# A two-layer transformer kernel on one core: smaller loads, a new instruction order, and query stacks transposed by DMA in the second layer

## The chip, the cores and the metric

The kernel runs on one core of one Trainium2 chip. The metric is the device time of one execution in microseconds. A core has TensorE (PE, matrix products and transposes into PSUM), VectorE (DVE), ScalarE (ACT), GpSimd (POOL) and SyncE (SP), which here only issues DMA transfers; each works through its own queue of instructions in order, and they wait for one another through semaphores.

## The reference

The input x is 8 blocks of 128 tokens by 128 features, the context is of the same shape. Two layers follow one another:

```
x = x + cross_attention_0(layernorm(x), ctx, mask[b])       # 16 heads of 8, mask of each block
x = x + bit_linear_ffn(layernorm(x))                         # 128 -> 512 (gate, up) -> 128, quantised
x = x + cross_attention_1(layernorm(x), ctx, mask shared)    # per-head weights, output bias
x = x + mixture_of_8_experts(layernorm(x))                   # all 8 computed, top 2 weighted
```

An attention computes q, k, v from the normalised x and from the context, the scores q k^T, sets masked ones to a very low value, and takes the softmax over keys and the product with v, then the output projection.

## The kernel before

A *unit* is one attention with the feed-forward part behind it, of one layer l and one block b: (l, b). There are 16, run in the order of UNIT_ORDER (line 71); n is a unit's place in it. Each unit is a list of steps such as `pe.max` or `dve.rk` (the engine, then the step), ATTENTION (line 75) and what STEPS adds for the layer. The function plan() (line 266) simulates the five queues with the costs in TIME (pitch and latency of each step), the buffer rings in SLOTS, the arrival times of loads in ARRIVES, and the ranks START and BIAS, and so fixes the order of each engine's instructions before the kernel is built. All engines then follow these orders, every step with waits for the steps it needs.

The scores need products of more precision than bf16 holds, so q and k are split into bf16 parts which lie side by side as a *stack*. For a unit these steps matter here:

- Keys: `pe.kv`, `act.kh`, `act.v`, `dve.rk`, `pool.km`, `pool.kl` fill kst (128 x 2048 bf16). `sp.ks` (line 566) turns it by a DMA transpose into kblk.
- Queries: layernorm (`dve.st`, `dve.ag`, `pool.pw`, `dve.nm`), `pe.xT`, `act.xT`, `pe.q`, `act.qh`, `dve.rq`, `pool.qm`, `pool.ql` fill qst (128 x 1024 bf16). `pe.qs` turns it in 8 TensorE transposes (line 708) into PSUM, and `act.qs` (line 850) copies it to qT.
- `pe.max` (lines 675, 677): the mask and the scores, 4 parts; `dve.max` (line 1063) takes their maximum over the keys. `dve.m1` to `dve.m3` write the maxima, split in three, into qst. `pe.qb` (again 8 transposes, line 708) and `act.qb` (line 850) make qmT, the shifted stack.
- `pe.exp` (lines 690, 692): shifted scores, with keys on the partitions; `act.exp` their exponential; `pe.pv`, `act.pv`, `pe.oT`, `dve.rd`, `dve.at`, `pe.aT`, `act.aT`, `pe.wo`, `dve.wo`: the output; `dve.fs` to `dve.fn`: the second layernorm.
- In layer 0, the quantised feed-forward; in layer 1 the experts: `pe.z` (line 826), `act.z`, `pe.y` (line 839), `dve.y` (line 1228), `pool.sum`, and `sp.out` (line 575), the store.
- `dve.mk` (lines 1043, 1044) casts the masks m0_i and m0T_i of one block.

Before the first unit, SyncE's queue holds the loads of x block 0, constants, x blocks 1 to 7, and the masks of blocks 0 and 1; ScalarE's queue holds the first layer's weights and the context. The rest of the loads stand behind the first four key transposes on SyncE (later_loads, line 535). SyncE issues everything in order, so a wait in its queue holds what stands behind it.

## Time and profile before

| | us |
|---|---|
| median of 3 runs (214.77 to 215.25) | 214.84 |
| profiled execution | 216.64 |
| its span, first to last instruction | 214.8 |
| TensorE busy | 196.6 |
| VectorE busy | 162.4 |
| ScalarE busy | 135.3 |
| GpSimd busy | 82.7 |

The span is what the trace covers; the 1.84 us by which the profiled execution is longer lie around it. Busy time of TensorE is from matmuls whose ends are modelled, so it shows whether the engine was supplied, not whether it ran at its peak.

### The profile page before, as it was taken

The numbers are of one execution on the slowest core, as the hardware profiler recorded it, in microseconds if no ns is written. First come the engines' busy times: TensorE is split into PE (matmuls) and PEld (weight loads), VectorE is DVE, ScalarE is ACT, GpSimd is POOL, SyncE is SP. The second block draws the span as 40 slices with busy tenths as digits, with TensorE's granted clock in tenths as the row PEclk, the third lists the DMA queues.
The fourth block names the chain that finished last, engine by engine and source line by source line (L and its number), as shares of the span: only waits on it lengthen the run. The fifth ranks groups of instructions, "written<-read, shape, count | busy, mean of one in ns | idle before, by whom it ended". The sixth has DMA issues, their size and how long they took to land.

```text
span 214.8 us, 6119 instructions
## 1 busy us (share of the span) xinstructions
PE 196.6 (92%) x2114; PEld 160.8 (75%) x2114; DVE 162.4 (76%) x608; ACT 135.3 (63%) x378; POOL 82.7 (38%) x197
## 2 busy tenths in 40 slices
PE   2487697999999999999999999999999999999992
PEld 0255474757766777777888988898979889999992
DVE  6458989999999999999987859966576736265225
ACT  3343466468868677766968579547955576566430
POOL 4494320432337544143520425438210604232532
PEclk9999889999999999999999999999999999999998
DMA  5849678504440724430080000400220000000000
GB/s 156 243 111 303 164 98 349 145 9 101 108 92 0 160 50 92 98 87 17 2 92 9 5 0 17 98 3 12 54 47 6 0 15 0 17 0 15 2 10 24
DMA packets 39747, 15.09 MB, mean 70 GB/s; under 512 B 34211, under 2 KB 38819, under 8 KB 39462
## 3 DMA queue, kind: packets, MB, share of 16 engines
q1 hardware_dynamic: 39142, 14.00, 27.7%
q10 hardware_dynamic: 576, 0.72, 1.0%
q8 instruction: 17, 0.28, 0.6%
q14 instruction: 12, 0.10, 0.1%
HBM read 5.80 MB, written 0.52 MB: 29 GB/s over the span
## 4 chain that ended last, share of the span: by engine, by line
PE 81%; DVE 7%; DMA 5%; issue 2%; SPq 2%; POOL 1%; ACT 1%; DVEq 0%; ACTq 0%
PE ps_B L826 14%; PE ps_A L839 12%; PE ps_O L756 7%; PE ps_B L690 7%; PE ps_A L675 6%; PE ps_B L692 6%; PE ps_Q L708 6%; PE ps_A L677 6%; DMA m0T_i<-in_mask0T 5%; PE ps_O L764 3%; PE ps_X L722 2%; PE ps_A L791 2%; PE ps_O L774 2%; PE ps_A L835 2%; PE ps_P L736 2%
## 5 line engine op out<-in xcount | busy, mean ns | idle before, releaser
L907 ACT ACTIVATE probs<-ps_B 128x512 f32<-128x512 f32 x64 | 36.5, 598 | 15.6 <-PE ps_B L692 14.8
L956 ACT ACTIVATE hid<-ps_B,b_sb 128x128 f32<-128x128 f32 x128 | 35.6, 378 | 15.3 <-PE ps_B L826 15.2
L1063 DVE TENSOR_REDUCE mx<-ps_A 128x4 f32<-128x512 f32 x64 | 42.0, 677 | 3.7 <-PE ps_A L677 3.7
L826 PE MATMUL ps_B<-mxT,w_sb 128*128 128x128 f32 x256 | 33.3, 278 | 0.0
L839 PEld LDWEIGHTS ps_A<-w_sb,hid 128*128 128x128 f32 x256 | 31.1, 192 | 0.6
L839 PE MATMUL ps_A<-w_sb,hid 128*128 128x128 f32 x256 | 31.2, 275 | 0.0
L826 PEld LDWEIGHTS ps_B<-mxT,w_sb 128*128 128x128 f32 x256 | 30.6, 192 | 0.5 <-issue 0.4
L654 POOL TENSOR_TENSOR yc<-yc 128x512 f32<-128x512 f32 (+2 forms) x21 | 17.3, 823 | 34.1 <-DVE yc L1228 33.0
L675 PE MATMUL ps_A<-m_b,id_b 128*128 128x512 bf16 x64 | 24.7, 385 | 2.4 <-DVE mx L1063 1.2
L692 PEld LDWEIGHTS ps_B<-qmT,kblk 118*128 118x128 bf16 x256 | 20.4, 100 | 8.6 <-issue 0.8
L692 PE MATMUL ps_B<-qmT,kblk 118*128 118x128 bf16 x256 | 25.5, 223 | 0.0
L677 PE MATMUL ps_A<-kblk,qT 112*128 112x256 bf16 x128 | 24.6, 273 | 0.0
L1228 DVE TENSOR_TENSOR yc<-ps_A,comb 128x512 f32<-128x512 f32 x16 | 11.0, 689 | 15.4 <-PE ps_A L839 15.3
L624 POOL CAST kst<-kr 128x128 bf16<-128x128 f32 x32 | 9.6, 328 | 30.1 <-DVE kr L1050 30.0
L708 PE MATMUL ps_Q<-id_b,qst 128*112 128x128 bf16 (+1 forms) x256 | 20.6, 225 | 0.3 <-ACT qT L850 0.2
L708 PEld LDWEIGHTS ps_Q<-id_b,qst 128*112 128x112 bf16 (+1 forms) x256 | 18.5, 136 | 2.4 <-issue 1.1
L590 POOL TENSOR_TENSOR ry<-hv,half 128x1 f32<-128x1 f32 x32 | 18.8, 586 | 2.7
L587 POOL TENSOR_SCALAR hv<-mv 128x1 f32<-128x1 f32 x32 | 7.1, 223 | 31.0 <-DVE mv L1111 27.0
L677 PEld LDWEIGHTS ps_A<-kblk,qT 112*128 112x128 bf16 x128 | 12.7, 99 | 8.4 <-issue 0.3
L722 PE MATMUL ps_X<-wkv_sb,ctx_sb 128*128 128x256 f32 x32 | 11.7, 450 | 6.8 <-DMA ctx_sb<-in_ctxT 4.0
L756 PE MATMUL ps_O<-probs,v_sb 128*9 128x128 f32 x512 | 17.0, 273 | 0.7 <-issue 0.7
L756 PEld LDWEIGHTS ps_O<-probs,v_sb 128*9 128x9 f32 x512 | 12.4, 90 | 3.1 <-issue 2.1
(135 smaller groups left out, 391.5 us busy)
## 6 DMA issues: line engine op xcount, KB each, us to landing
w_sb<-in_m1T SPq DMA_DIRECT2D x1, 1024.0 KB, 6.2
w_sb<-in_m2T SPq DMA_DIRECT2D x1, 1024.0 KB, 8.1
out_y<-out_sb SPq DMA_DIRECT2D x8, 64.0 KB, 1.5
x_sb<-in_x SPq DMA_DIRECT2D x1, 448.0 KB, 6.7
ctx_sb<-in_ctxT ACTq DMA_DIRECT2D x1, 448.0 KB, 5.5
m_i<-in_mask SPq DMA_DIRECT2D x1, 384.0 KB, 4.2
m0T_i<-in_mask0T SPq DMA_DIRECT2D x1, 384.0 KB, 5.0
kblk<-kst SPq DMA_TRANSPOSE x16, 3.7
```

The lines of the kernel that those rows point to most:

```text
L590: ends(pool.tensor_tensor(ry[:, k, b, :], hv[:, k, b, 0:1], half[:, :], ALU.pow), step)
L654: sum_part(pool.tensor_tensor(y[:, 0:w, :], y[:, 0:w, :], y[:, w:2 * w, :], ALU.add))
L675: pe.matmul(o[:, :].rearrange("p (h k) -> p h k", h=4), id_b[:, :], m, start=True, stop=False)
L677: mm = pe.matmul(o[:, 256 * (g % 2):256 * (g % 2) + 256].rearrange("p (j k) -> p j k", j=2), qT[0:ROWS, n % 2, g, :], kblk[0:ROWS, n % KSL ...
L692: mm = pe.matmul(o[:, P * (h % 4):P * (h % 4 + 1)], kblk[0:MROWS, n % KSLOTS, h % 2, h // 2, :], qmT[0:MROWS, n % 2, h // 2, :], start=Fal ...
L708: mm = pe.transpose(o[0:rows, g * P:(g + 1) * P], qst[:, n % 3, g, 0:rows], id_b[:, :])
L756: mm = pe.matmul(o[32 * j:32 * j + DH + 1, (h // 4) * P:(h // 4 + 1) * P], v_sb[:, n % KSLOTS, h, :], probs[:, n % 2, h, :], start=True, s ...
L826: mm = pe.matmul(psum("z", b, i)[:, c * P:(c + 1) * P], w1_sb[:, 4 * i + c, :], mxT[:, b % 2, :], start=True, stop=True)
L839: mm = pe.matmul(o[:, e * P:(e + 1) * P], hid[:, b % 2, c, :], w2_sb[:, c, :], start=False, stop=(c == 8 * i + 7))
L907: ends(act.activation(probs[:, n % 2, 4 * i:4 * i + 4, :], psum("exp", n, i)[:, :].rearrange("p (h k) -> p h k", h=4), ACT.Exp, scale=ATTN ...
L956: ins = act.activation(hid[:, b % 2, 4 * i + c, :], psum("z", b, i)[:, c * P:(c + 1) * P], ACT.Relu, bias=b1_sb[:, 4 * i + c:4 * i + c + 1])
L1063: ends(dve.tensor_reduce(mx[:, n % 2, 4 * i:4 * i + 4], psum("max", n, i)[:, :].rearrange("p (h k) -> p h k", h=4), AX.X, ALU.max), "dve.max")
```

## The change

1. Loads: x, context and masks come in more pieces (x and context: block 0, 1 to 3, 4 to 7; masks: 0, 1, 2 and 3, 4 to 7), with later pieces behind the first key transposes. The expert weights come in four pieces behind the fourth to seventh key transposes.
2. Second layer: `pe.qs`, `act.qs` and `pe.qb`, `act.qb` are replaced by `sp.qs` and `sp.qb`, each one DMA transpose of qst into qT or qmT (128 x 1024 bf16). The first layer keeps the TensorE form.
3. Rings: qst from 3 slots to 4, qT and qmT from 2 to 3. The memory comes from sharing: th and hr lie in wf_sb, the bias rows b2_sb and b2_f in yc.
4. The planner: other entries in TIME, ARRIVES, START (now one per unit and stage) and BIAS, LATENCY 0.04 for 0.1, and (0, 6) ahead of (1, 0), (0, 7) ahead of (1, 1).
5. At the start, the memsets of the second key slot and of the output bank leave the head of VectorE's queue (the first goes to GpSimd, the second behind `dve.rk` of unit 0), and some constants of GpSimd move behind `pool.kl` of unit 0.

```diff
-UNIT_ORDER = ((0, 0), (0, 1), (0, 2), (0, 3), (0, 4), (0, 5), (1, 0), (1, 1), (0, 6), (0, 7), (1, 2),
+UNIT_ORDER = ((0, 0), (0, 1), (0, 2), (0, 3), (0, 4), (0, 5), (0, 6), (1, 0), (0, 7), (1, 1), (1, 2),
               (1, 3), (1, 4), (1, 5), (1, 6), (1, 7))
+QUERY_STACK = ((("pe.qs", 1, "pool.ql"), ("act.qs", 1, "pe.qs")),
+               (("sp.qs", 1, "pool.ql"),))
+SHIFTED_STACK = ((("pe.qb", 1, "dve.m3"), ("act.qb", 1, "pe.qb")),
+                 (("sp.qb", 1, "dve.m3"),))
...
-    "pool.km": (0.53, 0.56), "pool.kl": (0.42, 0.49), "sp.ks": (2.5, 4.5), "pe.xT": (0.12, 0.32),
+    "pool.km": (0.53, 0.56), "pool.kl": (0.42, 0.48), "sp.ks": (1.7, 4), "pe.xT": (0.22, 0.34),
+    "pool.qm": (0.36, 0.42), "pool.ql": (0.4, 0.48), "pe.qs": (0.46, 0.53), "sp.qs": (1.3, 3.2),
+    "sp.qb": (1.3, 3.2), "act.qs": (0.5, 0.58), "pe.max": (0.45, 0.55), "dve.max": (0.6, 0.69),
...
-ARRIVES = {"dve.st": (3.3, 7.2), "pe.kv": (3.7, 7.2), "dve.mk": (7.0, 7.0, 15.0), "dve.ws": (17.0, 17.5, 18.0),
+ARRIVES = {"dve.st": (3.5, 6.5, 6.5, 6.5, 15.0), "pe.kv": (4.0, 6.5, 6.5, 6.5, 15.5),
+           "dve.mk": (8.2, 14.0, 18.0, 18.0, 25.0), "dve.ws": (19.0, 20.0, 21.0),
...
-            sp.dma_start(x_sb[:, 1:NB, :], x[1:NB].rearrange("b t d -> t b d")).then_inc(s_x, 16)
+            sp.dma_start(x_sb[:, 1:4, :], x[1:4].rearrange("b t d -> t b d")).then_inc(s_x, 16)
...
                 if n == 0:
+                    masks(1, 1, 2)
                     sp.dma_start(wo_sb[0][:, :], w0o).then_inc(s_wo, 16)
+                    sp.dma_start(x_sb[:, 4:NB, :], x[4:NB].rearrange("b t d -> t b d")).then_inc(s_x4, 16)
+                    sp.dma_start(ctx_sb[:, 4:NB, :], ctxT[:, 4:NB, :]).then_inc(s_ctx4, 16)
                 if n == 1:
-                    masks(1, 2, NB)
+                    masks(2, 2, 4)
...
                 if n == 2:
+                    masks(3, 4, NB)
+                if n == 3:
...
-                if n == 3:
-                    sp.dma_start(w1_sb[:, :, :], m1T).then_inc(s_moe, 16)
-                    sp.dma_start(w2_sb[:, :, :], m2T).then_inc(s_moe, 16)
+                if n == 4:
...
+                if n in (3, 4, 5, 6):
+                    part = slice(4 * (n - 3), 4 * (n - 3) + 4)
+                    sp.dma_start(w1_sb[:, part, :], m1T[:, part, :]).then_inc(s_moe, 16)
+                    sp.dma_start(w2_sb[:, part, :], m2T[:, part, :]).then_inc(s_moe, 16)
...
-            masks(0, 0, 2)
+            masks(0, 0, 1)
...
+                if name == "qs":
+                    after(sp, "pool.ql", n)
+                    if n >= TSLOTS:
+                        after(sp, "pe.max", n - TSLOTS)
+                    if b >= 2:
+                        wait_landed(sp, b - 2, "qs")
+                    sp.dma_start_transpose(qT[:, n % TSLOTS, :, :], qst[:, n % QSLOTS, :, :].rearrange("p g c -> p (g c)")
+                                           ).then_inc(landed["qs"][b % 2], 16)
+                if name == "qb":
+                    after(sp, "dve.m3", n)
+                    if n >= MSLOTS:
+                        after(sp, "pe.exp", n - MSLOTS)
+                    if b >= 2:
+                        wait_landed(sp, b - 2, "qb")
+                    sp.dma_start_transpose(qmT[:, n % MSLOTS, :, :], qst[:, n % QSLOTS, :, :].rearrange("p g c -> p (g c)")
+                                           ).then_inc(landed["qb"][b % 2], 16)
...
-            act.dma_start(ctx_sb[:, 1:NB, :], ctxT[:, 1:NB, :]).then_inc(s_ctx, 16)
+            act.dma_start(ctx_sb[:, 1:4, :], ctxT[:, 1:4, :]).then_inc(s_ctx, 16)
...
             zeros(qst[:, 0, :, :]).then_inc(qst_zero, 1)
-            zeros(kst[:, 1, :, :, :]).then_inc(kst_zero, 1)
-
-            dve.memset(banks["O"][0][:, :], 0.0).then_inc(bank_zero, 1)
```

## Rows read from the trace of the kernel before

**Rows 1.** The page, busy time of each engine

```profile
PE 196.6 (92%) x2114; PEld 160.8 (75%) x2114; DVE 162.4 (76%) x608; ACT 135.3 (63%) x378; POOL 82.7 (38%) x197
```

**Rows 2.** Stretches: length, busy by engine, granted clock, DMA share, GB/s

```profile
0.00:10.00 10.00, 3.56 (x7) 1.68 (x7) 4.82 (x15) 3.70 (x10) 4.72 (x20) 1.00 0.68 196
10.00:20.00 10.00, 7.10 (x40) 4.53 (x41) 6.37 (x23) 4.07 (x13) 8.04 (x22) 1.00 0.74 203
20.00:30.00 10.00, 8.38 (x61) 5.61 (x60) 9.88 (x35) 4.66 (x12) 3.57 (x7) 0.83 0.59 134
30.00:40.00 10.00, 8.15 (x121) 6.11 (x121) 8.49 (x20) 5.47 (x11) 1.22 (x4) 1.00 0.95 262
40.00:100.00 60.00, 58.59 (x686) 43.12 (x684) 59.35 (x237) 44.51 (x110) 24.90 (x68) 1.00 0.36 80
100.00:160.00 60.00, 60.00 (x693) 51.89 (x694) 46.23 (x186) 44.12 (x129) 23.36 (x51) 1.00 0.17 30
160.00:209.00 49.00, 49.00 (x511) 46.28 (x500) 23.74 (x90) 28.72 (x97) 15.23 (x24) 1.00 0.03 7
```

The engines stand in the order PE, PEld, DVE, ACT, POOL.

**Rows 3.** The chain that ended last, over the start: start, us, what

```profile
2.73 6.34 DMA m0T_i<-in_mask0T
...
12.83 1.33 SPq L566
...
14.95 5.04 DMA m0T_i<-in_mask0T
```

**Rows 4.** Stretch from 111 us as in rows 2; instructions of line 826

```profile
111.00:209.00 98.00, 98.00 (x1039) 89.64 (x1037) 60.36 (x238) 64.00 (x203) 33.99 (x65) 1.00 0.09 20
...
L826 PE MATMUL ps_B<-mxT,w_sb x256: 270/275/377, 111.4 to 204.5; 128*128 128x128 f32 x128
```

**Rows 5.** Timelines of SyncE, ScalarE, VectorE and TensorE in the first 20 us

```profile
7.36 1.67 SPq L566 DMA_TRANSPOSE kblk<-kst  x1
9.09 0.56 SPq L538 DMA_DIRECT2D wo_sb<-in_w0o  x1
...
7.81 0.49 ACT L847 ACTIVATE qst<-ps_P 128x384 bf16<-128x384 f32 x1 [0.95 <-PE ps_P L736]
...
9.92 0.27 DVE L1056 TENSOR_TENSOR qr<-ps_P,qst 128x128 f32<-128x128 f32 x1
...
14.31 0.61 PE L675 MATMUL ps_A<-m_b,id_b 128*128 128x512 bf16 x1
...
19.90 0.39 PE L675 MATMUL ps_A<-m_b,id_b 128*128 128x512 bf16 x1 [0.72 <-ACT qT L850]
```

**Rows 6.** Instructions that touch kblk: ns min/median/max; DMA to landing

```profile
L566 SPq DMA_TRANSPOSE kblk<-kst x16: 1328/1604/2865, 7.4 to 153.5; - x16
...
DMA to landing us min/median/max: 3.6/3.7/5.8
```

**Rows 7.** DMA issues of x: out<-in, count, KB, us to landing

```profile
x_sb<-in_x SPq DMA_DIRECT2D x1, 448.0 KB, 6.7
...
x_sb<-in_x SPq DMA_DIRECT2D x1, 64.0 KB, 2.5
```

**Rows 8.** Query stacks: one on the chain; line 708 from 111 us; line 850

```profile
112.49 0.45 PE ps_Q L708 x8
...
111.00:209.00 98.00, 5.49 (x72) 5.01 (x72) 1.00 0.09 20
...
L850 ACT COPY qT<-ps_Q x16: 578/585/655, 13.7 to 157.6; 112x512 int32<-112x512 int32 x16
```

**Rows 9.** One stretch, columns as in rows 2

```profile
25.00:28.60 3.60, 3.60 (x28) 2.78 (x27) 3.56 (x12) 1.78 (x3) 3.31 (x7) 0.53 0.24 70
```

**Rows 10.** Waits of SyncE's queue: us in total, times, longest

```profile
SPq L575 <- POOL out_sb L657: 85.8, 7, 21.7
```

More of the change, by code:

```diff
@@ L118 @@
     ("dve.fn", 1, "pool.fp"),
-)
+) for l in range(2)]
 STEPS = (
-    (("dve.mk", 1),) + ATTENTION + (
+    (("dve.mk", 1),) + ATTENTION[0] + (
         ("dve.q0", 1, "dve.fn"),
@@ L262, in steps_of @@
+GROUP = {name: k for k, names in enumerate(STAGES) for name in names.split()}
 def steps_of(n):
@@ L412, in build @@
         b1_sb = sb("b1_sb", [P, ZCH])
[L413 to L414 removed]
+        yc = sb("yc", [P, 2, E, P])
+        b2_sb, b2_f = [yc[:, i, :, :].rearrange("p e o -> p (e o)") for i in range(2)]
         b2_h = sb("b2_h", [P, E * P], BF16)
@@ L661, in _, with query_stack_ready, shifted_stack_ready @@
         def _(pe):
+            def query_stack_ready(n):
+                if units[n][0] in BY_DMA:
+                    wait_landed(pe, units[n][1], "qs")
+                else:
+                    after(pe, "act.qs", units[n][1])
+            def shifted_stack_ready(n):
+                if units[n][0] in BY_DMA:
+                    wait_landed(pe, units[n][1], "qb")
+                else:
+                    after(pe, "act.qb", units[n][1])
             def maxima_scores(n, i):
                 l, b = units[n]
+                if n == 0 and i == 0:
+                    pe.wait_ge(id_ready, 1)
                 if i == 0:
-                    after(pe, "act.qs", n)
+                    query_stack_ready(n)
                     wait_landed(pe, n)
@@ L701, in turn, with stack @@
                 ends(pe.transpose(o, src, idn), "pe." + name)
-            def stack(name, n, rows):
-                wait_free(pe, name, n)
-                o = psum(name, n)[:, :].bitcast(BF16)
+            def stack(name, n, b, rows):
+                wait_free(pe, name, b)
+                o = psum(name, b)[:, :].bitcast(BF16)
                 for g in range(GROUPS):
-                    mm = pe.transpose(o[0:rows, g * P:(g + 1) * P], qst[:, n % 3, g, 0:rows], id_b[:, :])
+                    mm = pe.transpose(o[0:rows, g * P:(g + 1) * P], qst[:, n % QSLOTS, g, 0:rows], id_b[:, :])
                 ends(mm, "pe." + name)
@@ L885, in _ @@
                     after(act, "pe.q", n)
-                    if n >= 3:
-                        after(act, "pe.qb", n - 3)
+                    if n >= QSLOTS and units[n - QSLOTS][0] in BY_DMA:
+                        wait_landed(act, units[n - QSLOTS][1], "qb")
+                    elif n >= QSLOTS:
+                        after(act, "pe.qb", units[n - QSLOTS][1])
                     elif n:
```

227 lines of the change are left out of this document (122 added, 105 removed), and 7 rows, old and new, of the table START.

## The prediction

> **What bounds the kernel now.** I read four views in this order. First the page's busy times: TensorE 92%, VectorE 76% [rows 1]. An average over stages says little, so next the busy time by stretch [rows 2]. Three stages stand out. From 0 to 40 us TensorE works 27.2 of 40 us (3.56 + 7.10 + 8.38 + 8.15), so 12.8 us are idle: the pipeline is filling, and VectorE is idle for 10.4 us too. From 40 to 100 us VectorE is busy 59.35 of 60 and TensorE 58.59: VectorE leads by a little, TensorE is close behind. From 100 us to 209 us TensorE is busy all the time, and VectorE falls to 46.23 of 60 and then 23.74 of 49. The last 5.8 us are VectorE's sums of the last block and its store; the change leaves them alone. The third view is the chain of work that ended last, over the start [rows 3]: it runs through the two transposed-mask loads (6.34 and 5.04 us), each time into VectorE's mask casts, and then through the second key transpose. So the end is set by: how late the start is, plus VectorE's work until about 111 us, where the expert matmuls begin [rows 4], plus TensorE's work from there on (98.00 of 98.00 us busy [rows 4]).
>
> The profiled execution took 216.64 us, 1.84 more than its span of 214.8. The shown runs have a median of 214.84. I make the sum on the span and take the same difference off both: the 1.84 us outside the span are the same before and after. What three runs can tell from no change is about 0.2%, 0.43 us.
>
> **Term 1, the start: -3.0 us (0 to -4.4).** Before, x and the context come in a piece of 448 KB each behind the first blocks, and the masks of two blocks (128 KB each) stand behind the big x piece on SyncE's queue. The transposed mask lands at 2.73 + 6.34 = 9.07 us [rows 3], and VectorE stands at the cast until then; behind it in VectorE's queue are the statistics of unit 1 and the query remainder of unit 0 (dve.rq, 9.92 us [rows 5]), and GpSimd waits for that. The change puts 64 + 69 + 192 + 64 + 64 KB on SyncE's queue and 128 + 64 + 64 + 192 KB on ScalarE's: 901 KB in place of 1541. At the same rate 7 us of loading become about 4, so the cast can run near 6.5 us, before unit 0's query is ready (its copy runs 7.81 to 8.30 us [rows 5]). The remainder then starts at 8.3 in place of 9.92. From 9.92 to the first scores at 14.31 us [rows 5] it took 4.39 us, in which GpSimd also did work of unit 1. So the first scores move to 12.7 us at the latest, and not ahead of 11.1, where the first key transpose has landed (7.36 + 3.7 [rows 5, 6]). That is 1.6 to 3.2 us.
>
> Unit 1: its scores started at 19.90 us, on a query stack [rows 5]. Behind the first key transpose SyncE now issues five loads in place of one (unit 1's mask pair, wo, the rest of x, the rest of the context). At 0.56 us each [rows 5] that is 2.8 us, so the second key transpose can be issued at 9.03 + 2.8 = 11.8 us (12.83 before) and lands at 15.5: 4.4 us before 19.90. Unit 2: its mask pair (now 128 KB each, not 384) has its second half issued at about 13.8 and lands 2.5 us (a 64 KB piece [rows 7]) to 5.0 us (384 KB [rows 3]) later, 16.3 to 18.8 us against 20.0: 1 to 4 us. The three gains follow one another and do not add; VectorE carries the shift through, being full from 20 us on (9.88 of 10 [rows 2]). I take 3.0 and keep 0 and 4.4 as ends. The memsets of the second key slot and of the output bank leave the head of VectorE's queue, for GpSimd and for a place behind the first key remainder; GpSimd also clears three query slots in place of two, while it waits for statistics anyway. Both are inside the term.
>
> A rule of the Trainium skill speaks against this part: DMA: Bandwidth & Descriptors, section "Rules for kernel authors", tells to coalesce many small transfers into one large one. The trace agrees that a piece of 64 KB is no cheap one, 2.5 us against 6.7 for 448 KB [rows 7]; by the rule term 1 would be nothing and the time 209.1 us. I side with the rows, since what waits here is the first piece and not the last byte.
>
> **Term 2, stacks off TensorE after 111 us: -4.05 us (same at both ends).** The change removes TensorE's eight transposes for each query stack (qs) and shifted stack (qb) of the eight second-layer units: 16 stacks of 32. One takes 0.45 us of the chain [rows 8]. After 111 us stand 72 transposes [rows 8], 9 stacks, all of the second layer (unit (0,7) is through by then). TensorE is busy 98.00 of 98.00 us there, so this work comes off the end: 9 x 0.45 = 4.05.
>
> **Term 3, the seven other stacks: -1.2 us (0 to -3.15).** They lie before 111 us, where VectorE leads. TensorE saves 7 x 0.45 = 3.15 us there, but that counts only if expert matmuls (first at 111.4 us [rows 4]) can be drawn forward into the hole, which takes a second-layer unit that is ready. The new order starts the second layer one place later. I take 1.2, a little over a third.
>
> ScalarE loses 16 copies of 0.585 us [rows 8]; it is idle a quarter to two fifths of the time from 40 us on [rows 2], so this counts nothing by itself.
>
> **Term 4, the transposes by DMA: +1.0 us (0 to +4.4).** No query stack goes by DMA in this trace. The nearest row is the key stack: issue 1.60 us on SyncE, landing 3.6 to 5.8 us after, median 3.7, for 16 blocks of 128x128 [rows 6]. A query stack has 8. Its landing lies between 1.8 (half of 3.6) and 5.8 us; I take 3.2, nearer to the whole since a 64 KB load of any kind has 2.5 us [rows 7]. The replaced path is 0.45 us on TensorE and 0.585 on ScalarE [rows 8], 1.0 us. So each stack comes 2.2 us later (0.8 to 4.8), a unit 4.4 us later. What hides it is the backlog of expert matmuls of the units before; with three slots (qT and qmT had two, qst three, now four) two units may be under way. If one unit at the change of stages finds no cover, it costs 4.4; I take about a quarter. SyncE's queue has room: three issues a unit are 1.6 + 0.8 + 0.8 = 3.2 us (a query stack's issue at half a key stack's), in (209 - 111)/8 = 12 us. Transfer share is 0.17 and less after 100 us [rows 2].
>
> **Term 5, the queues ordered anew: -1.5 us (+1.85 to -3.25).** The orders of all engines come from the planner with other costs, due times and unit order. What an order can win is TensorE's idle time after 30 us: 1.85 us in 30 to 40 and 1.41 in 40 to 100 [rows 2], 3.25 together. As much as the first could be lost again. In between lies -1.5, on the winning side because the old table held 2.5 and 4.5 us for the key transpose, which took 1.6 and 3.7 [rows 6].
>
> **Nothing:** the expert weights in four pieces, behind the fourth to the seventh of 16 key transposes, while the first expert matmul starts at 111.4 us [rows 4]; buffers that share memory (th, hr over the loaded weights; b2's rows over yc): their users are ordered already. **The clock:** from 25.0 to 28.6 us the granted clock was 0.53 [rows 9], the lower of the two levels (1.2 of 2.4 GHz) for most of it, after a start in which TensorE was busy about half. That is 1.7 us of TensorE's time, while VectorE was full as well (3.56 of 3.6). I count 0; it can come or go by 1.7.
>
> Sum: -3.0 - 4.05 - 1.2 + 1.0 - 1.5 = -8.75. Span 206.05, profiled execution 207.9, median 214.84 - 8.75 = **206.1 us**.
>
> **Rivals.**
> A. *The start does not move, the stacks pay.* SyncE's five issues stand before the second key transpose, and VectorE's own work (weight sums and casts, then all maxima) sets the pace whatever arrives. For: 9.88 of 10 busy from 20 us. Against: 3.6 us of VectorE idle in 10 to 20 [rows 2]. Without term 1: 209.1 us; 208.5 to 212 by the other terms' ends. The skill's rule above comes out here.
> B. *The new orders pack more.* VectorE's 10.4 us idle in the first 40 shrink by more than 4.4 and expert work fills all holes: -4.4 - 4.05 - 3.15 - 3.25 = -14.85, 200.0 us; 196 to 202.
> C. *DMA stacks are not hidden.* TensorE has less backlog in the middle than I think; two units pay in full, +8.8 in term 4 in place of +1.0: 213.9 us; 212 to 214.4.
> D. *SyncE's queue in its order turns the gain round (slower).* SyncE waits 85.8 us in seven waits of output stores for GpSimd's sum, up to 21.7 at a time [rows 10]. Before, only key transposes stood beside these; now up to 16 query stacks share the queue. A stack queued behind a store that is not yet due stops TensorE. Each costs what the sum is late, and its price decides from (8.75 + 1.0)/16 = 0.6 us a stack on; at 0.9 us each, +14.4 in place of +1.0, 219.5 us. Against: in the trace the stores are planned far ahead and SyncE is else idle.
>
> **Chances.** Forecast 0.60 (own range 202.5 to 208.5). A 0.13, B 0.12, C 0.05, no difference 0.02, D 0.08. All but D and the even case are faster: 0.90, 0.02, 0.08. The range that leaves out D, the even case, C and the far ends of A and B is 200 to 210.5.
>
> **What will show it.** The first cast of m0T near 6.5 us, first scores before 12.7, unit 1's before 17. No ScalarE copies to qT or qmT for the second layer (16 in place of 32 in all), 128 transposes on TensorE. Key-stack rows beside 16 query transposes with landing 2 to 4 us. TensorE busy without a break from 105 us to the last expert matmul, which should end near 200. It is wrong if TensorE shows waits for qT or qmT by DMA over 1 us in sum, if VectorE's first 20 us are as idle as before, or if SyncE's waits for out_sb stand ahead of a late stack.

## The result, and the profile after

The changed kernel takes **221.8 us** (median of four executions, 220.72 to 223.42) where the kernel before takes 214.84: the ratio is 1.033, with a 95% interval of 1.026 to 1.039. It is slower by 7.0 us; 206.1 was forecast, and a range of 200 to 210.5. The profiled execution took 221.96 us with a span of 220.2. The profiled execution of the kernel before (216.64 us, mean granted clock 0.987) was slower than all its other runs, which have 0.995 to 1.00 wherever the clock is listed, so the two spans differ by less than the medians do.

The page's busy times, against [rows 1]:

```profile
PE 197.0 (89%) x1986; PEld 154.8 (70%) x1986; DVE 165.3 (75%) x607; ACT 128.1 (58%) x362; POOL 83.5 (38%) x198
```

TensorE has 128 matmuls fewer and ScalarE 16 copies fewer, so the stacks did leave them. Yet TensorE's busy time is no shorter, 197.0 for 196.6, in a span 5.4 us longer. The stretches, in the columns of [rows 2], say where both come from:

```profile
10.00:20.00 10.00, 8.94 (x55) 5.95 (x53) 5.38 (x15) 4.80 (x14) 5.14 (x15) 1.00 0.90 211
20.00:30.00 10.00, 6.90 (x33) 3.76 (x32) 7.77 (x25) 1.35 (x3) 1.63 (x4) 0.68 0.56 137
30.00:40.00 10.00, 9.18 (x112) 6.88 (x112) 7.32 (x32) 7.12 (x17) 4.97 (x12) 0.98 0.47 115
40.00:100.00 60.00, 52.88 (x582) 36.51 (x580) 55.76 (x208) 38.57 (x95) 21.94 (x58) 0.97 0.58 122
```

From 20 to 30 us TensorE gets through 33 matmuls where it got through 61 [rows 2]. From 40 to 100 us it is idle for 7.1 us (1.4 before) and VectorE for 4.2 (0.65 before): the stage in which VectorE led, and no idle time was to be had, now has gaps in both engines. From 111 us to 209 TensorE is still nearly full:

```profile
111.00:209.00 98.00, 97.19 (x1004) 85.23 (x997) 66.70 (x258) 62.32 (x201) 37.39 (x76) 1.00 0.28 54
```

The last stage did not become short of work; it began late. The first expert matmul runs at 113.3 us, 1.9 later than in [rows 4], with more of the stages before it still undone: the last matmul of the same line starts at 211.9 us (204.5 before).

The chain of work that ended last, over the start (start, us, what), against [rows 3]:

```profile
11.96 3.01 SPq L603
15.01 0.58 SPq L561
15.64 0.47 SPq L563
16.15 0.43 SPq L575
16.62 0.43 SPq L575
17.10 0.43 SPq L575
17.64 6.21 DMA kblk<-kst
23.94 0.59 PE ps_A L746
...
37.72 2.67 DMA yc<-in_mb
40.42 0.68 DVE b_h L1067
```

The mask loads are off the chain, as they should be. In their place stands the third key transpose. SyncE issues it at 17.64 us, directly behind a mask pair and the three loads of the feed-forward weights (L575, 256 KB each); it lands 6.21 us later, where 3.7 was the median before [rows 6]. The late landing is not new: before, the third key transpose stood behind the same three loads and had the 5.8 us of [rows 6], issued at 19.00 and landed at 24.8 us (now at 23.85):

```profile
19.00 2.87 SPq L566 DMA_TRANSPOSE kblk<-kst  x1
```

What the change did move is the load of the bias rows (L584), from behind the third key transpose to behind the fourth. TensorE's timeline names the wait (last bracket: idle before, and what ended it), and VectorE's names a second one, for the bias rows:

```profile
23.94 0.59 PE L746 MATMUL ps_A<-m_b,id_b 128*128 128x512 bf16 x1 [2.57 <-DMA kblk<-kst]
```

```profile
40.42 0.68 DVE L1067 CAST b_h<-yc 3x1024 bf16<-3x1024 f32 x1 [3.01 <-DMA yc<-in_mb]
```

Two more rows of TensorE's timeline, the first scores and the first shifted scores. They stood at 14.31 us [rows 5] and, from the same view of before, at 22.38 (unit 1's first scores are at 18.79 us, 19.90 before):

```profile
15.24 0.63 PE L746 MATMUL ps_A<-m_b,id_b 128*128 128x512 bf16 x1
...
31.98 0.38 PE L761 MATMUL ps_B<-m0T_b,id_b 128*128 128x512 bf16 x1
```

The second one is the big shift. The new order of TensorE puts twelve groups of first scores (units 0, 1 and 2) ahead of the first shifted stack; the old one put that stack behind six. So the late key transpose of unit 2 now stands in front of unit 0's second half.

Then the clock. Six 5-us windows, columns as in [rows 2], the last column but two being the granted clock:

```profile
20.00:25.00 5.00, 2.39 (x12) 1.02 (x11) 4.88 (x19) 0.49 (x1) 1.63 (x4) 0.86 1.05 249
25.00:30.00 5.00, 4.51 (x22) 2.75 (x21) 2.89 (x7) 0.86 (x2) 0.00 (x0) 0.50 0.08 26
30.00:35.00 5.00, 4.18 (x41) 3.10 (x42) 4.92 (x22) 3.80 (x9) 1.87 (x5) 0.96 0.25 57
35.00:40.00 5.00, 5.00 (x72) 3.78 (x70) 2.40 (x12) 3.32 (x9) 3.10 (x7) 1.00 0.70 173
40.00:45.00 5.00, 2.37 (x41) 1.87 (x42) 4.58 (x8) 2.29 (x7) 0.00 (x0) 0.91 0.93 188
45.00:50.00 5.00, 5.00 (x47) 3.23 (x36) 3.50 (x11) 2.28 (x4) 0.26 (x2) 0.75 0.39 106
```

At 0.50 the granted clock is the lower level, 1.2 of 2.4 GHz, through all of 25 to 30 us, and it falls a second time behind TensorE's 2.6 us wait, which ends at 42.75 us. A window of 5 us at a mean clock c does the work of 5c us, so these six lose 5 x (0.14 + 0.50 + 0.04 + 0 + 0.09 + 0.25) = 5.1 us; in the profiled execution of before, the same sum is 5 x 0.34 = 1.7 (its window from 25 to 30 had 0.66). The time lost is at most this, since TensorE is idle for part of it. The lower clock also explains why TensorE's busy time did not shrink: the 33 matmuls from 20 to 30 us each took longer.

Last, the new transposes and the key transposes (duration on SyncE in ns, min/median/max; then landing):

```profile
L613 SPq DMA_TRANSPOSE qT<-qst x8: 1231/1232/1250, 81.4 to 165.6; - x8
...
DMA to landing us min/median/max: 2.7/2.8/3.6
```

```profile
L603 SPq DMA_TRANSPOSE kblk<-kst x16: 1457/2034/4266, 7.3 to 154.7; - x16
...
DMA to landing us min/median/max: 3.6/4.6/7.2
```

A query stack lands after 2.8 us (3.2 was taken) and takes 1.23 us to issue (0.8 was taken). The key transposes are what changed: 4.6 us in the median for 3.7, and up to 4.27 us to issue for 2.87 [rows 6].

Four candidates are left, and they can act together: the loads in pieces (what stands in front of a key transpose), the latency of the DMA stacks, the orders, and the clock that follows a stall.

### The profile page after: what moved, and what is told of

It is laid out like the page before. It is cut to its first block, busy times and chain, and to the rows that moved or that the text cites. A ratio compares the mean times of both kernels' runs of the same rounds, so it can differ in the third digit from the quotient of the medians.

```text
span 220.2 us, 5861 instructions
## 1 busy us (share of the span) xinstructions
PE 197.0 (89%) x1986; PEld 154.8 (70%) x1986; DVE 165.3 (75%) x607; ACT 128.1 (58%) x362; POOL 83.5 (38%) x198
## 4 chain that ended last, share of the span: by engine, by line
PE 57%; DVE 16%; DMA 8%; issue 6%; SPq 6%; POOL 4%; ACT 2%; ACTq 0%; DVEq 0%
PE ps_B L899 13%; PE ps_A L912 12%; DMA kblk<-kst 5%; PE ps_O L829 4%; PE ps_A L746 4%; PE ps_A L748 4%; PE ps_B L761 3%; PE ps_B L763 3%; DVE mx L1137 3%; SPq L603 3%; PE ps_O L837 2%; PE ps_Q L779 2%; PE ps_O L847 2%; PE ps_A L908 1%; POOL ry L643 1%
## 5 line engine op out<-in xcount | busy, mean ns | idle before, releaser
L746 PE MATMUL ps_A<-m_b,id_b 128*128 128x512 bf16 x64 | 26.2, 410 | 3.1 <-DMA kblk<-kst 2.6
L748 PE MATMUL ps_A<-kblk,qT 112*128 112x256 bf16 x128 | 26.1, 287 | 0.0
L748 PEld LDWEIGHTS ps_A<-kblk,qT 112*128 112x128 bf16 x128 | 13.3, 104 | 9.7 <-issue 2.2
L829 PE MATMUL ps_O<-probs,v_sb 128*9 128x128 f32 x512 | 17.7, 281 | 0.1
L681 POOL CAST kst<-kr 128x128 bf16<-128x128 f32 x32 | 8.7, 300 | 21.0 <-DVE kr L1122 21.0
L920 ACT ACTIVATE oT_sb<-ps_O 128x512 f32<-128x512 f32 x16 | 9.6, 602 | 11.8 <-PE ps_O L829 11.7
L829 PEld LDWEIGHTS ps_O<-probs,v_sb 128*9 128x9 f32 x512 | 12.7, 92 | 3.0 <-issue 1.8
L691 POOL CAST qst<-qr 128x256 bf16<-128x256 f32 x16 | 6.4, 398 | 20.8 <-DVE qr L1130 20.7
```

The lines of the kernel that those rows point to most:

```text
L746: pe.matmul(o[:, :].rearrange("p (h k) -> p h k", h=4), id_b[:, :], m, start=True, stop=False)
L748: mm = pe.matmul(o[:, 256 * (g % 2):256 * (g % 2) + 256].rearrange("p (j k) -> p j k", j=2), qT[0:ROWS, n % TSLOTS, g, :], kblk[0:ROWS, n ...
L829: mm = pe.matmul(o[32 * j:32 * j + DH + 1, (h // 4) * P:(h // 4 + 1) * P], v_sb[:, n % KSLOTS, h, :], probs[:, n % 2, h, :], start=True, s ...
```

## The experiments

In all of these the orders of the five queues are written out as lists where that is needed, so that one part can be changed while the rest stays in place.

### The square: loads, stacks and orders apart

**e3_old_loads** is the changed kernel with every load as before (the sizes, the queue and the place of [rows 5]); orders and DMA stacks are the new ones.

```
-            sp.dma_start(x_sb[:, 1:4, :], ...)
+            sp.dma_start(x_sb[:, 1:NB, :], ...)
...
-                    masks(2, 2, 4)
+                    masks(1, 2, NB)
...
-                if n == 3:
+                if n == 2:     # mask1, layer-1 weights, biases
...
-                if n in (3, 4, 5, 6):   # w1_sb, w2_sb in four pieces
+                if n == 3:              # whole
```

> The changed kernel with all loads cut and placed as in the kernel before; orders of the five queues, stacks by DMA and rings as changed. Theory L (the pieces and their places do the harm, as the second key transpose is now issued behind five loads and the third behind five): 215 to 218 us. Rival O (the new orders do the harm, whatever the loads are): 220 to 223 us. If the pieces do what they are for, the start is later here and it is slower than 221.8.

Measured: 217.48 us, ratio 1.0138 (1.0097 to 1.0179). The loads cost 4.3 of the 7.0 us. The other 2.6 stand without them, and they stand in the middle stage (columns of [rows 2]):

```profile
40.00:100.00 60.00, 54.85 (x636) 38.91 (x642) 56.76 (x216) 40.03 (x97) 24.76 (x62) 1.00 0.46 100
```

TensorE 54.85 of 60 us and VectorE 56.76, at full clock: gaps in both, made by order or by latency.

The start of e3 says what the loads' cost is not. Its third key transpose stands behind the same three weights and behind larger masks, and lands no earlier (16.68 + 7.06 = 23.74 us), so unit 2's first scores come at 23.83 us, in the changed kernel at 23.94. But VectorE's cast of the bias rows runs at 36.61 us without a wait, in the changed kernel at 40.42:

```profile
16.68 4.93 SPq L596 DMA_TRANSPOSE kblk<-kst  x1
```

```profile
23.83 0.38 PE L739 MATMUL ps_A<-m_b,id_b 128*128 128x512 bf16 x1 [1.36 <-DVE m0T_b L1107]
```

```profile
36.61 0.80 DVE L1058 CAST b_h<-yc 3x1024 bf16<-3x1024 f32 x1
```

**e4_pe_stacks** is the changed kernel with the second layer's stacks back on TensorE and ScalarE, each placed where SyncE's step stood.

```
-BY_DMA = (1,)
+BY_DMA = ()
...
-                  (("sp.qb", 1, "dve.m3"),))
+                  (("pe.qb", 1, "dve.m3"), ("act.qb", 1, "pe.qb")))
```

> The changed kernel with the second layer's query stacks back on TensorE and ScalarE, each put into these queues at the place where the planner starts the DMA transpose; the relative order of everything else and all loads as changed. If the DMA stacks save TensorE 16 x 0.45 = 7.2 us and are hidden, this is 226 to 229 us. Rival T (DMA stacks come too late and cost more than they save): below 221 us, down to 215.

Measured: 230.04 us, 1.0713 (1.067 to 1.0756). **e13_new_order_only** is the same with the old loads too:

> The new queue orders alone: old loads, all stacks on TensorE (put in where the planner starts the transposes). It closes the square of orders and stacks at old loads: old orders 214.8 (TensorE) and 220.1 (DMA), new orders 217.5 (DMA). If loads and orders add (4.3 us of e3): 225 to 226.5 us. If the new orders are no worse than the old ones by themselves: 215 to 217 us, and e4's 230 comes from the pieces.

Measured: 227.06 us, 1.0577 (1.0516 to 1.0637). Inside the new orders the DMA stacks are worth 9.6 us (227.06 to 217.48) and 8.2 with the new loads; the new orders alone, under TensorE stacks, cost 12.2 us. A caution on that size: these orders were made for stacks by DMA, and the steps put back into them stand where SyncE's stood, not where a planner would place them.

**e5_old_order_dma** turns it about: the orders and loads of before, with the second layer's stacks by DMA (and the start's moved memsets and the longer rings of the change, which make no difference by themselves, e15 below).

```
-               (("pe.qs", 1, "pool.ql"), ("act.qs", 1, "pe.qs")))
+               (("sp.qs", 1, "pool.ql"),))
```

> The queue orders, unit order and loads of the kernel before, with only the second layer's stacks by DMA: 16 stacks are taken out of TensorE's and ScalarE's queues and put into SyncE's by the planner's ready times; rings of 4, 3 and 3 slots. If the stacks pay (terms 2 to 4 of the prediction): 214.84 - 4 to 6 = 209 to 211 us. Rival T: 215 to 222 us.

Measured: 220.1 us, 1.0223 (1.0168 to 1.0277). In the old orders the same stacks cost 5.3 us. TensorE's waits show a part of it (in total, times, longest):

```profile
PE ps_A L784 <- DMA qT<-qst: 3.8, 4, 1.6
PE ps_B L799 <- DMA qmT<-qst: 3.3, 4, 1.1
```

| orders | loads | stacks on TensorE | stacks by DMA |
|---|---|---|---|
| old | old | 214.84 | 220.1 |
| new | old | 227.06 | 217.48 |
| new | new | 230.04 | 221.8 |

The stacks' worth has the opposite sign in the two orders, so it isn't a property of the stacks. The new loads under the old orders were not run.

### What the stacks' latency costs

**e11_old_zero** and **e12_new_zero** are e5 and the changed kernel with the latency taken out: second-layer scores read a fixed tile of zeros, so they are not the reference's, and wait only for the step that filled the query slot. The transposes still run.

```
-                    wait_landed(pe, units[n][1], "qs")
+                    after(pe, "pool.ql", n)
...
-                    wait_landed(pe, units[n][1], "qb")
+                    after(pe, "dve.m3", n)
...
-    qT[0:ROWS, n % TSLOTS, g, :], kblk[...]
+    (fixed[0:ROWS, g, :] if l else qT[0:ROWS, n % TSLOTS, g, :]), kblk[...]
```

> e5 (old orders, old loads, DMA stacks) with the latency of the stacks taken off: in the second layer TensorE multiplies a fixed tile of zeros in place of qT and qmT, and waits for the step that fills the stack, not for its transpose; the transposes are still issued and land in their own tiles (the second layer's scores are thus not the reference's). VectorE's first step of the maxima waits for the query transpose, since it writes into its source. If e5's loss is latency (7.2 us saved, 12.5 lost): 207 to 209.5 us. If something else in e5 costs (traffic of the transposes, start of the queues, rings): 213 us or more.

> The changed kernel with the latency of the DMA stacks taken off in the same way as in e11. If the changed orders hide the stacks (e4 says they are worth 8.2 us there): 220.5 to 221.8 us, and the loss lies in the orders and loads of the first layer. If the latency of the stacks is the loss: 212 to 216 us.

Measured: e11 212.9 us, 0.9903 (0.9884 to 0.9922); e12 222.18 us, 1.0336 (1.03 to 1.0372). In the old orders the latency costs 220.1 - 212.9 = 7.2 us. In the new orders it costs nothing: 222.18 and 221.8 overlap. So the changed kernel hides its transposes, and its loss is not theirs.

e11 also prices the work that was taken off TensorE. With no latency at all, 16 stacks fewer bring 214.84 - 212.9 = 1.9 us, not 5.25. TensorE's two late stretches in e11:

```profile
100.00:160.00 60.00, 58.87 (x626) 48.94 (x622) 47.63 (x191) 40.41 (x121) 23.34 (x51) 1.00 0.35 70
160.00:209.00 49.00, 47.54 (x464) 44.97 (x463) 24.13 (x87) 26.96 (x92) 16.93 (x26) 1.00 0.08 19
```

Where [rows 2] have 60.00 of 60.00 and 49.00 of 49.00, there are now 2.6 us of gaps. With the transposes gone TensorE seems to run ahead of what the other engines have ready; which of them it waits for was not followed up.

### Which loads

**e1_early_bias** loads the bias rows one key transpose earlier, **e14_ffn_bias_moved** does that and loads the feed-forward weights one key transpose later, and **e10_gap_loads** puts all later loads behind the third key transpose.

```
e1, e14:         if n == 2:
+                    sp.dma_start(b2_sb[0:3, :], mb2...)     # was under n == 3
e14:
-                if n == 1:   # wg, wu, wd, 256 KB each
+                if n == 2:
e10:
-                if n == 3: / if n == 4: / if n in (3, 4, 5, 6):
+                all of it under n == 2, w1_sb and w2_sb whole
```

> The changed kernel with one load moved: the 12 KB of expert output bias (needed by VectorE's first b_h cast, which waited 3.01 us and ran at 40.42 us) are issued behind the third key transpose instead of the fourth. Theory S (the changed kernel loses at the start, and a start that is late stays late): the 3.0 us wait goes and most of it reaches the end, 221.8 - 2 to 3 = 218.8 to 219.8 us. Rival T (the loss comes from the DMA stacks of the second layer, the start is caught up later): within 0.5 us of 221.8.

> The changed kernel with two loads moved behind the third key transpose, small enough to be through before the fourth: the three feed-forward weights (768 KB, until now in front of the third key transpose) and the 12 KB of expert output bias. Theory K (the harm of the new loads is two stalls of TensorE, 2.6 us on the third key transpose and 2.6 us behind VectorE's bias cast, each followed by a stretch at the lower clock): granted clock back to 0.99 and 217 to 218.5 us, the old loads' 217.5. Rival (the loads harm otherwise, or the orders need them where they are): 220.5 us or more, at whatever clock.

> The changed kernel, orders and DMA stacks as they are, with all loads that stood behind the fourth to seventh key transposes (second layer's weights, shared masks, biases, the expert weights in two whole pieces) moved behind the third, where SyncE's queue stands idle from 22.95 to 32.78 us. No key transpose is then queued behind a load after the third. If loads in front of the key transposes (landing 4.6 us in the median, up to 7.2) and the late bias (3.0 us of VectorE) cost the middle stage: 216 to 218.5 us, as with the old loads (217.5). If it is the order of the queues alone: 220.5 us or more.

Measured: e1 220.77 us (1.0296, 1.0247 to 1.0345), e14 218.25 (1.0148, 1.0105 to 1.019), e10 221.72 (1.0279, 1.0215 to 1.0343). e1 takes VectorE's 3.0 us wait away and gives 1.0 us in the median, inside the spread of the two kernels. e14 gives 3.6 of the loads' 4.3. Its SyncE timeline, where the transpose now stands ahead of the weights:

```profile
15.47 0.47 SPq L563 DMA_DIRECT2D m0T_i<-in_mask0T  x1
16.12 2.12 SPq L603 DMA_TRANSPOSE kblk<-kst  x1
18.29 0.57 SPq L576 DMA_DIRECT2D wf_sb<-in_wg  x1
```

It starts 1.5 us earlier and takes 2.12 us to issue in place of 4.13, landing at 20.4 us, and no TensorE wait for kblk is left in the list of waits.

VectorE's order is the same in e3, the changed kernel, e1, e14 and e10, so one and the same instruction can be compared in all five. The table has VectorE's maxima, from its timelines: the start in e3, and how much later (+) or earlier (-) each of the others is. The profiled executions took 217.29, 221.96, 219.70, 218.94 and 222.95 us; for e1 it is the fastest of four, for e10 the slowest.

| maxima of | e3, at us | changed | e1 | e14 | e10 |
|---|---|---|---|---|---|
| unit 1, last | 22.51 | -1.1 | 0.0 | -0.8 | -0.4 |
| unit 2, third | 28.36 | +0.6 | -0.2 | -0.8 | -0.4 |
| unit 3, first | 39.45 | +3.7 | -0.2 | -0.9 | +2.7 |
| unit 5, first | 56.53 | +3.6 | -0.1 | -0.8 | +4.6 |
| unit 6, first | 68.14 | +4.6 | +1.1 | +0.6 | +4.6 |
| unit 7, first | 81.73 | +4.6 | +2.3 | +1.6 | +5.6 |
| unit 15, last | 168.02 | +4.6 | +2.3 | +1.6 | +5.6 |

The steps are few and sharp. The changed kernel is 1.1 us ahead at 22 us and loses that at the third key transpose, where e3 waits too. (e12, which has its loads and orders, repeats both long waits: TensorE 2.4 us for kblk, VectorE 2.8 us for the bias rows.) The late bias rows then cost 3.1 us, and 1.1 us more are lost between units 5 and 6. e1 has no late bias and keeps pace with e3 to 0.2 us until 56 us, so the early loads in pieces neither gain nor cost; but between units 5 and 6 it loses 1.3 us, as e14 does (1.4). There the pieces of the expert weights stand ahead of the seventh and eighth key transposes. From e1:

```profile
55.28 0.58 SPq L591 DMA_DIRECT2D w_sb<-in_m1T  x1
55.90 0.43 SPq L592 DMA_DIRECT2D w_sb<-in_m2T  x1
56.44 4.19 SPq L603 DMA_TRANSPOSE kblk<-kst  x1
```

```profile
ACT kst L942 <- DMA kblk<-kst: 2.1, 2, 1.4
```

```profile
58.19 0.29 DVE L1122 TENSOR_TENSOR kr<-ps_X,kst 128x128 f32<-128x128 f32 x1 [1.10 <-ACT v_sb L920]
```

The transposes land 6.0 and 7.2 us after their issue (4.3 and 3.9 in e3). kst has two slots, so ScalarE cannot write the next key stack before an earlier one has landed; it waits 2.1 us, and VectorE waits behind it. e3 has neither wait. The last step of e1, e14 and e10, 1.2, 1.0 and 1.0 us, lies between 78 and 84 us, where their granted clock falls (0.66, 0.76 and 0.80 from 80 to 85 us, 1.00 in e3 and in the changed kernel). And what e14 gains over e1 in these two executions is the lead of 0.8 us that it does not lose at the third key transpose.

e10 moves the same trouble down the queue. Behind 2 MB of expert weights the fourth key transpose takes 6.17 us to issue, and TensorE then stands 4.49 us:

```profile
28.82 0.43 SPq L587 DMA_DIRECT2D w_sb<-in_m1T  x1
29.30 0.44 SPq L588 DMA_DIRECT2D w_sb<-in_m2T  x1
31.70 6.17 SPq L599 DMA_TRANSPOSE kblk<-kst  x1
```

```profile
41.11 0.59 PE L742 MATMUL ps_A<-m_b,id_b 128*128 128x512 bf16 x1 [4.49 <-issue]
```

The profile names no releaser here; that it is the transpose is read from the times (31.70 + 9.3, this kernel's longest landing, is 41.0). In the table e10 has lost 4.6 us by then, and nothing between units 5 and 6, where it has no pieces.

### Orders

**e8_unit0_first** moves five of TensorE's 361 steps: unit 0's shifted stage goes ahead of unit 2's first scores, as in the old order.

```
-  max.1.2 max.1.3 max.2.0 max.2.1 xT.4.0 q.4.0 qs.3.0 max.2.2 max.2.3 qb.0.0 wm.0.0 qb.1.0 exp.0.0 ...
+  max.1.2 max.1.3 qb.0.0 exp.0.0 exp.0.1 exp.0.2 exp.0.3 max.2.0 max.2.1 xT.4.0 q.4.0 qs.3.0 ...
```

> The changed kernel with one stretch of its orders altered: unit 0's shifted stack, its four shifted-score groups and its last two steps of the maxima stand ahead of unit 2's first scores on TensorE, VectorE and ScalarE. If the start is lost because unit 0 stands behind unit 2's key transpose (landed at 23.85 us): first shifted scores at 22 to 24 us in place of 32.2, and 3 to 7 us off the end, 215 to 219 us. Rival (the rest of the order, tuned to the planner's own start, gives it back): 220 to 223 us.

Measured: 225.7 us, 1.0452 (1.0389 to 1.0515), worse by 3.9. The first shifted scores come at 25.18 us in place of 31.98, but unit 2's scores now stand behind unit 0's shifted ones, and VectorE waits 3.66 us for them. Its longest TensorE wait is VectorE's step behind the bias cast:

```profile
29.16 0.69 DVE L1183 TENSOR_REDUCE mx<-ps_A 128x4 f32<-128x512 f32 x1 [3.66 <-PE ps_A L794]
```

```profile
PE ps_O L818 <- DVE attn L1218: 4.1, 1, 4.1
```

The fourth key transpose is issued at 35.13 us in place of 32.78, so the bias rows behind it come later too, and their cast waits 3.72 us until 43.48. A single group moved by hand in a fixed order meets the next fixed thing.

**e9_searched_new**, **e6_searched_dma** and **e7_searched_pe** keep everything of a kernel but its orders: e9 the changed kernel, e6 e5, e7 the kernel before. Single steps were moved as long as a model of the fixed orders (durations and landings of these traces, with several delays per hand-over) got shorter. In e7, 107 of TensorE's 377 steps, 231 of VectorE's 546 and one of SyncE's stand elsewhere; in e9, 92 of 361, 227 of 546 and 8 of 40. TensorE's start in the kernel before and in e7:

```
-  qs.0.0 q.1.0 max.0.0 max.0.1 xT.2.0 max.0.2 q.2.0 max.0.3 kv.3.0 qs.1.0 xT.3.0 max.1.0 q.3.0 max.1.1 ...
+  qs.0.0 q.1.0 max.0.0 xT.2.0 max.0.1 q.2.0 max.0.2 qs.1.0 max.0.3 kv.3.0 max.1.0 xT.3.0 max.1.1 qb.0.0 ...
```

> The changed kernel (its loads in pieces, its unit order, its DMA stacks) with only the queue orders moved as in e6. Theory F: 208 to 213 us, so that nothing but the order of the queues stands between the changed kernel and a gain. If the pieces of the loads are at fault beyond the order: 215 us or more and over 3 us above e6.

> The kernel of e5 (old unit order, old loads, DMA stacks in the second layer), with the queue orders moved step by step until the list is short under three release delays (0.06, 0.12 and 0.18 us) and a key transpose of 3.7 us: an order with slack, not with a best case. Theory F (the stacks by DMA are worth 5 to 7 us, and both e5 and the changed kernel lose them to orders that leave them no room): 208 to 212 us. Rival T (a second-layer unit by DMA is too late in any order): 215 us or more.

> The kernel before, untouched but for the queue orders, which are moved in the same way as in e6; all stacks on TensorE. It tells what orders alone are worth and is the partner of e6: e7 less e6 is what the DMA stacks bring when both have room. Theory F: 210 to 213 us, and 3 to 6 us above e6. Rival T: at or below e6.

Measured: e9 215.1 us (1.0012, 0.9982 to 1.0042), e6 214.65 (0.9982, 0.9959 to 1.0005), e7 **213.29** (0.9914, 0.9884 to 0.9944). e9 is the changed kernel, loads in pieces, DMA stacks, rings and all, and its order alone takes 6.7 us off it. Its stretch from 20 to 30 us (the profiled execution, 216.95 us, is among the slowest of its ten):

```profile
20.00:30.00 10.00, 7.75 (x66) 4.84 (x64) 9.78 (x33) 3.30 (x10) 2.81 (x8) 1.00 0.96 225
```

66 matmuls for 33, VectorE 9.78 of 10, and the clock at its upper level. e7 beats both kernels, with TensorE stacks and old loads. With the orders freed on both sides, DMA stacks are 1.4 us slower than TensorE stacks (214.65 and 213.29). But e6 has the change's start and rings and e7 has not; against e16 below, which has them (213.8), it is 0.85 us, and the two intervals touch. Each order is the best that one search found, so neither figure bounds the stacks' worth.

**e17_searched_new_moved** is e9 with the two loads moved as in e14:

> e9 (the changed kernel with searched orders, 215.1 us) with the two loads moved as in e14. Its orders were searched with the loads in their changed places, so that it may wait for the feed-forward weights on VectorE instead. If the third key transpose held it too: 212.5 to 214 us. If not: 214.5 to 216.5 us.

Measured: 214.96 us, 1.0002 (0.9988 to 1.0017), no gain over e9, though the third key transpose lands at 20.9 us in place of 24.7. The loads in pieces cost 4.3 us under the new order. Under the searched orders nothing of that is to be seen: 215.1 us with pieces and 214.65 with whole loads (e6), each in an order of its own; the same searched order with both kinds of loads was not run.

### The start by itself

**e15_before_start** is the kernel before with the change's moved memsets and longer rings; **e16_searched_pe_start** is e7 with the same.

```
+QSLOTS = 4
+TSLOTS = 3
+MSLOTS = 3
```

> The kernel before (its orders, unit order and loads, all stacks on TensorE) with only the changed kernel's start of the queues (memsets off VectorE's head, GpSimd's constants later) and its rings of 4, 3 and 3 slots. The first products with v stood at 27.9 and 28.5 us in e5 and e11, with the same orders and loads, against 30.03 before. If the start does that: 212.5 to 213.5 us. If it came from elsewhere in e5: 214.5 to 215 us.

> The searched orders of e7 (stacks on TensorE) with the start and the rings of e15. If both gains add: 211 to 212.5 us, and the best version of all has no DMA stack in it. If the start gives nothing on top: 213 to 213.5 us.

Measured: e15 215.03 us over 12 executions (1.0002, 0.9991 to 1.0014), e16 213.8 (0.9947, 0.9934 to 0.9961). e15's first product with the values starts at 28.4 us, 1.6 earlier than in the profile of before, and the times are equal all the same. The traces say why. e15 has the orders of before, so one and the same instruction can be compared: VectorE's maxima start 0.3 us later at 15 to 17 us, at the same time at 23 to 25 us, and 1.2 us earlier from 35 us to the end (spans 213.6 and 214.8). Between them lies one window, of before and of e15:

```profile
25.00:30.00 5.00, 5.00 (x36) 3.59 (x34) 4.96 (x18) 3.06 (x8) 3.31 (x7) 0.66 0.22 61
```

```profile
25.00:30.00 5.00, 5.00 (x75) 3.78 (x74) 4.97 (x18) 3.30 (x9) 3.32 (x7) 1.00 0.23 63
```

So the moved start and the longer rings are worth nothing, and the lead is that of the granted clock: the profiled execution of before had a stretch at the lower level, e15's had none. It prices such a stretch, 1.7 us by the mean clock, at 1.2 us. e16 was expected below e7 and is not.

## Why the prediction was wrong, step by step

The terms were added up, and the parts do not add. With the loads taken last, the stacks and orders together (terms 2 to 5) were to bring -5.75 us and cost +2.6 (e3), a miss of 8.4; the loads (term 1) were to bring -3.0 and cost +4.3, a miss of 7.3.

**Term 1, the start, -3.0 (0 to -4.4): failed.** The step that failed is the last one, "VectorE carries the shift through". The working followed the masks and the first two key transposes, and not the third key transpose, nor the loads that were moved behind a later one. Three things were missed.

First, the first transposed mask lands 2.5 us earlier (2.69 + 3.9 = 6.6 us for 9.07), but unit 0 does not gain by it. The first scores came at 15.24 us, not 12.7. The masks were cast at 9.69 us (6.5 was forecast), because the new order of VectorE puts statistics and remainders of units 1 to 3 first; the query remainder was done at 8.05, as said, but the new orders spent the lead. GpSimd has two statistics chains ahead of the query (8.53 to 10.29 us), ScalarE has a query split, a key split and an xT copy ahead of the turned query (its copy to qT runs at 13.58 us, 13.67 before, though TensorE's transposes for it start at 11.72, 0.84 earlier than before), and TensorE has unit 2's query and the fourth context product ahead of the scores (13.83 and 14.39 us). Unit 1's scores are 1.1 us early.

Second, that lead of 1.1 us ends at the third key transpose. It landed at 24.8 us before, at 23.74 with the old loads in the new orders and at 23.85 in the changed kernel: 768 KB of feed-forward weights stand in front of it in all three. The "5.8 at most" of [rows 6] was this very transpose.

Third, the bias rows' load went behind one more key transpose and was late for VectorE by 3.0 us. It had not been priced at all, and it is the largest part of the loads' +4.3 us (3.1 in the table). e14 gives 3.6 of the 4.3 us back by moving both loads; of these two only the bias had been moved by the change.

Under TensorE's stacks the same loads cost +3.0 us (e13 to e4). The prediction's own sign of being wrong was there: VectorE is idle for 9.5 of the first 20 us, 8.8 before. Rival A's first half, that the start does not move, came true. Its range of 208.5 to 212 us does not come out of the other terms' ends, which reach from 204.4 to 217.0.

**"Nothing: the expert weights in four pieces": failed.** They were checked against the first expert matmul only, which they do not hold up. They stand ahead of the key transposes of units 6 and 7, and these cost 1.1 to 1.4 us between units 5 and 6 in the changed kernel, e1 and e14.

In the Trainium skill, DMA: Bandwidth & Descriptors, section "Two DMAs through the same engine are not ordered", says that within one queue of a DMA engine descriptors start in order. The trace agrees: the transposes behind loads landed after 6.2 us here and up to 9.3 in e10, against 3.6 with nothing ahead. The rule weighed in the prediction, that small transfers should be coalesced, was not what decided: with every early piece in place e1 keeps pace with e3, within 0.4 us, until 56 us. What decided is which transpose, and which consumer, stood behind a load.

**Terms 2 and 3, the stacks off TensorE, -4.05 and -1.2: mechanism right, size wrong.** The count of instructions is as said (128 matmuls, 16 copies). What they are worth is -1.9 us (e11), with latency at zero. The step that failed is "TensorE is busy 98.00 of 98.00 us there, so this work comes off the end". An engine that is full is the bound only as long as nothing else is right behind it: e11 has 2.6 us of new gaps on TensorE after 100 us. And 1.9 us is with the 1.0 us path through TensorE and ScalarE gone as well.

**Term 4, latency, +1.0 (0 to +4.4): right for this kernel, and wrong as a price.** The landing was well placed (2.8 us for 3.2). In the new orders the latency is hidden (e12). In the old ones it costs 7.2 us, beyond the upper end, so the "backlog of expert matmuls" was no cover there. That the new orders had to be built round it, and so carry its price, is an argument. Rival C had the right mechanism for e5 and is not what slowed the changed kernel.

**Term 5, the orders, -1.5 (+1.85 to -3.25): wrong as a term of its own.** Under DMA stacks the new orders bring -2.6 us, inside the range; under TensorE's stacks they cost 12.2. It was bounded by TensorE's idle time in the kernel before, on the tacit assumption that a planner with measured durations does no worse. The bound holds for what an order can win, not for what it can lose. At old loads the new orders leave 5.15 us of TensorE and 3.24 us of VectorE idle from 40 to 100 us (e3), and other orders for the very same work take 6.7 us off (e9). The 2.6 us that they win under DMA stacks (220.1 to 217.48) are less than the 5.3 that the stacks had cost. Whether the planner's shortened hand-over time (0.04 us for 0.1) is to blame was not tried. It is an argument only, as is the remark that its plan gives SyncE's plain loads no time and a key transpose behind them no delay.

**The clock, counted as 0 (up to 1.7 either way): mis-sized.** It lost up to 5.1 us for 1.7 before. The lower level came with TensorE's stall of 2.57 us that ended at 23.94, and again after its stall of 2.63 us that ended at 42.75. In e3 only the window from 25 to 30 us is low (0.66), as before, and so it is in e1, which has the 768 KB in the same place: the deeper fall comes where TensorE reaches the third key transpose early and stands longest. One such stretch cost 1.2 us at the end where it was 1.7 by the mean clock (before and e15). If every lost microsecond costs as much, an estimate, the 5.1 of the changed kernel are 3.6 us of its time, and the 1.7 of e3 are 1.2 of the 2.6 us by which it stands above the kernel before. The usual executions of the kernel before, at 0.995 to 1.00, pay almost nothing of this.

**Rival D, SyncE's order: right side, wrong mechanism.** SyncE waits 47.7 us for GpSimd's sum at the stores, not 85.8, and its waits ahead of query stacks are for the query itself, which no queue could have had earlier; e12 leaves nothing for a late stack to cost. The harm in SyncE's queue was a load behind one transpose more (the bias rows, at 37.7 us) and plain loads ahead of key transposes (at 53 to 60 us).

The account of the 7.0 us, by the square: DMA stacks in the old orders +5.3, the new orders -2.6, the new loads +4.3. The other way round the square it is +12.2, -9.6 and +4.3. The loads' term is the same on both only because it comes last; ahead of the stacks it is +3.0. The range was too narrow for its own terms, too: their unfavourable ends add up to 217.0 us, not 210.5, and even that lies below 221.8. **What stays open:** which short waits make up the middle stage's gaps in the new orders, and what the new loads would do under the old orders.

## What to carry to other kernels

Price every load twice: by what is issued behind it in its queue, and by the transpose that it now stands behind. 12 KB moved behind one more key transpose cost 3 us, which is more than splitting all loads gained. Follow each gain to the first thing that the change does not move, here the third key transpose. Where two kernels have the same orders, compare the start of the same instruction in both: the loss shows as a few sharp steps. In a kernel whose orders are fixed, the worth of moving work to another unit is not a number of its own: measure it with the latency set to zero (what it can bring in that order) and with the orders redone, here 1.9 us and no gain. And an engine that is 100% busy late in a kernel bounds the gain only up to the next engine's readiness.

## What the runs showed of the hardware

- A DMA transpose's time depends on what its queue still has in flight, in the issue as well as in the landing: 1.46 us and 3.6 at best, 4.13 and 6.2 behind 256 KB of masks and 768 KB of weights, 4.93 and 7.1 behind 768 KB of each (e3), 6.17 and 9.3 behind 2 MB (e10). SyncE is held for all of the issue.
- A transpose of a 128x1024 bf16 stack takes 1.23 us to issue and 2.8 to land; of one twice that size 1.6 and 3.7. Half the work saves a quarter.
- In the changed kernel a stall of about 2.6 us on TensorE is followed by time at the lower clock level, in both places where it occurs: a mean of 0.54 over 23.9 to 31.0 us and of 0.66 over 43 to 48 us. In e10, 40 to 45 us, behind its stall of 4.5 us, it is 0.50. Such a stall is not needed for it: before, the clock was 0.53 from 25.0 to 28.6 us [rows 9] where TensorE's waits from 20 us on were at most 0.94 us. The four executions of the changed kernel follow their mean clock roughly: 220.72 us at 0.981, 221.63 at 0.974, 221.96 at 0.977, 223.42 at 0.967.
- VectorE's page in the Trainium skill, VectorE: DVE Perf Modes, section "Rules for kernel authors", advises TensorE for a 128x128 transpose where a PSUM destination is acceptable, and the DMA transpose otherwise. The runs are in keeping with it: with orders made for each, TensorE's version is faster by 1.4 us (e7 and e6), or by 0.85 with the same start and rings (e16 and e6).
